# Reading each stack of queries or keys back from DRAM in one transfer of overlapping runs instead of two

## The chip, the cores and the metric

The kernel runs on one core of a Trainium2 chip. The metric is the device time of one execution in microseconds (us). Three runs of the kernel before give a median of 3047.06 us (3043.91 to 3050.0).

## What is computed

Two transformer-like blocks and two feed-forward stacks over one sequence of 2048 tokens with 128 channels. Cut to what matters here:

```python
def _attn(x, wq, wk, wv, wo, bq, bk, bv, bo):          # 16 heads of 8 dimensions, causal
    q, k, v = (x @ wq + bq), (x @ wk + bk), (x @ wv + bv)   # split into heads
    att = einsum('bhqd,bhkd->bhqk', q, k) * hd ** (-0.5)
    att = softmax(where(causal, att, -inf))
    return einsum('bhqk,bhkd->bhqd', att, v) @ wo + bo

x = x + _L0_attn_a_ref(_layernorm(x), ...)   # cumulative sums, stage a
x = x + _L0_ffn_ref(_layernorm(x), ...)      # 2 layers: causal attention, 8 experts (top 2), stage f
x = x + _L0_attn_b_ref(_layernorm(x), ...)   # attention without a mask, stage b
x = x + _L0_ffn_ref(_layernorm(x), ...)      # 2 layers again, stage g
```

There are five attention stages: f0, f1, b, g0, g1.

## The kernel before, in words

The 2048 tokens are worked on in 4 chunks of 512 (`CHUNKS`, `CH`). A projection computes q, k and v of a chunk. To have float32-like scores from bf16 products, each q and k is split into three bf16 parts, high, mid and low (0, 1, 2), and six products of parts are added: these are six groups of 8 rows (`HD`), stacked in 48 partitions of `m.q_stack` and `m.k_stack`, so that one matmul contracts over all of them. There are two such stacks, in partitions 0 to 47 (half b = 0, even heads) and 64 to 111 (half b = 1, odd heads). Row 48 of each is the shift row: in q_stack the negative row maximum, in k_stack ones.

The parts reach the stacks through DRAM, because the rows have to change partition. `write_part` (lines 670 to 678, and 936 to 945; `EarlyProjection.write` in the second layers) writes one part of q or k of a chunk into its slots of `q_parts` or `k_parts`; `Q_SLOTS` and `K_SLOTS` say which part is in which slot, and a part that stands in two slots is written to both by one transfer. The DRAM tensor has the slots outermost, then the 8 dimensions, the 16 heads, the 2048 tokens. `load_stacks` (lines 680 to 694 and 947 to 961; `EarlyProjection.load` from line 1241) reads a chunk and half of q and then of k back. Before, each takes two transfers: the four slots (32 partitions), then two slots again (16 partitions). Both count on one semaphore, and `arrived = 32 * (m.layers + 1)` is what TensorE waits for.

```python
queue.wait_ge(written[k][c % 2], 16 * 3 * (c // 2 + 1))
at = HALF * b
for n, first in ((SLOTS, 0), (AGAIN, again)):
    queue.dma_start(stack[at:at + n * HD, c, :, :],
                    dram.rearrange("r (hp b) s -> r b hp s", b=2)[first * HD:(first + n) * HD, b, :, cols])\
        .then_inc(arrived[b][c], 16)
    at += n * HD
```

Who issues what is written out by hand. In the full projections (`project_qkv` for f0 and b, `project_behind` for g0) SP issues the writes of all chunks and, for half 0, the loads of chunks 0 and 1; ACT issues chunk 0, half 1; GpSimd (POOL) chunk 1, half 1. The loads of chunks 2 and 3 are issued in the attention stage: in f0 and g0 by SP between its shifts (half 0) and by POOL between its masks (half 1), in b by both ahead of everything else. In the second layers (f1, g1, `EarlyProjection`) SP and POOL issue chunks 0 and 1 during the experts of the layer before, between SP's loads of the combine rows (line 2713), and chunks 2 and 3 in the attention stage. ScalarE reuses a slot of `parts` for chunk c only when the writes of chunk c - 2 have landed (`act.wait_ge(written[k][c % 2], ...)`, line 819), and SP, ACT and POOL wait for the same semaphores before a load.

In an attention stage TensorE works in the order of a planner (`Plan`): scans (line 1696) whose maxima VectorE takes (line 1856), a turn of the maxima (line 1716) and a shift on SP for every group of queries (lines 1928 and 1933), then scores (line 1734), exp on ScalarE (line 1804) and products with v (line 1755). TensorE waits for q_stack and k_stack of a chunk at their first use, and for the shift of a group at its first scores. In f0, f1, g0 and g1 the first four groups need chunk 0 alone; in b the first two groups are scanned against the keys of all four chunks, chunk after chunk.

Of the kernel before, what the change touches and what calls it, by code (L numbers as in the profile page):

```python
# [16 lines left out]
S = 2048  # L17
TILES = S // P
CH = 512
CHUNKS = S // CH  # L20
TPC = CH // P
HEADS, HD = 16, 8
# [11 lines left out]

Q_SLOTS = [0, 1, 2, 0]
K_SLOTS = [2, 1, 0, 0]
SLOTS = len(Q_SLOTS)
Q_AGAIN, K_AGAIN = 0, 1  # L40
AGAIN = 2
STACK = (SLOTS + AGAIN) * HD
PAIRS = HEADS // 2
HALF = P // 2
SHIFT_ROW = STACK
VD = HD + 1
# [9 lines left out]
class Steps:  # L56
# [5 lines left out]
    def __call__(self, instruction):  # L62
        self.n += 1
        instruction.then_inc(self.sem, 1)
        self.engine.wait_ge(self.sem, self.base + self.n)


def by_dim(ap):
# [559 lines left out]
def project_qkv(nc, m, n, buffers, layer=None, first_rows=None):  # L628
# [6 lines left out]
    with ExitStack() as ctx:  # L635
# [34 lines left out]
        def write_part(sp, c, k, part):  # L670

            dram, parts_of = ((m.q_dram, Q_SLOTS), (m.k_dram, K_SLOTS))[k]
            places = [g for g, of in enumerate(parts_of) if of == part]
# [6 lines left out]
        def load_stacks(queue, c, b):  # L680

            cols = slice(c * CH, (c + 1) * CH)
            for k, (stack, dram, arrived, again) in enumerate(((m.q_stack, m.q_dram, m.q_in, Q_AGAIN),
                                                               (m.k_stack, m.k_dram, m.k_in, K_AGAIN))):
                queue.wait_ge(written[k][c % 2], 16 * 3 * (c // 2 + 1))
                if c == CHUNKS - 1:
                    queue.wait_ge(v_ready, CHUNKS)
                at = HALF * b
                for n, first in ((SLOTS, 0), (AGAIN, again)):
                    queue.dma_start(stack[at:at + n * HD, c, :, :],  # L690
                                    dram.rearrange("r (hp b) s -> r b hp s", b=2)[first * HD:(first + n) * HD, b, :, cols])\
                        .then_inc(arrived[b][c], 16)
                    at += n * HD

        @block.gpsimd
        def _(pool):
            if first_rows:
                first_rows.powers(pool, BACK, 2)
            else:
                inverse_root(nc, pool, m, m.rstd[:, :], tmp[:, 0, :], var_ready, rstd_ready, 1)  # L700
            m.clear(pool, "finish", "experts", "rows", "w2")
            buffers.pad(nc, m)
            load_stacks(pool, 1, 1)

        @block.sync
        def _(sp):
            for c in range(CHUNKS):
                for part, ready in enumerate((high_ready, mid_ready, low_ready)):
                    for k in range(2):
                        sp.wait_ge(ready, 2 * c + k + 1)  # L710
                        write_part(sp, c, k, part)
                    if part == 0 and 0 < c <= EARLY:
                        load_stacks(sp, c - 1, 0)
# [87 lines left out]
        def _(act):  # L801
# [13 lines left out]
            for c in range(CHUNKS):  # L815
                for k in range(2):
                    act.wait_ge(mixed if mixing else qk_ready, 2 * c + k + 1)
                    if c >= 2:
                        act.wait_ge(written[k][c % 2], 16 * 3 * (c // 2))
                    if mixing:  # L820
                        nc.scalar.activation(parts[:, c % 2, k, 0, :], projected(c, k), ACT.Copy)\
                            .then_inc(high_ready, 1)
                    else:
                        nc.scalar.activation(parts[:, c % 2, k, 0, :], projected(c, k), ACT.Identity, bias=bias[k])\
                            .then_inc(high_ready, 1)
                if c == 1:
                    load_stacks(act, 0, 1)
                if c + 2 < CHUNKS:
                    copy_chunk(c + 2)
                for k in range(2):  # L830
                    act.wait_ge(rest_ready, 2 * c + k + 1)
                    nc.scalar.activation(parts[:, c % 2, k, 1, :], rest[:, k, :], ACT.Copy).then_inc(mid_ready, 1)
# [73 lines left out]
def project_behind(nc, m, n, buffers, layer, first_rows, attended, finish):  # L906

    src, end = m.x, CHUNKS - 1
    with ExitStack() as ctx:
# [26 lines left out]
        def write_part(sp, c, k, part):  # L936

            dram, parts_of = ((m.q_dram, Q_SLOTS), (m.k_dram, K_SLOTS))[k]
            places = [g for g, of in enumerate(parts_of) if of == part]
# [7 lines left out]
        def load_stacks(queue, c, b):  # L947

            cols = slice(c * CH, (c + 1) * CH)
            for k, (stack, dram, arrived, again) in enumerate(((m.q_stack, m.q_dram, m.q_in, Q_AGAIN),  # L950
                                                               (m.k_stack, m.k_dram, m.k_in, K_AGAIN))):
                queue.wait_ge(written[k][c % 2], 16 * 3 * (c // 2 + 1))
                if c == end:
                    queue.wait_ge(v_ready, CHUNKS)
                at = HALF * b
                for n, first in ((SLOTS, 0), (AGAIN, again)):
                    queue.dma_start(stack[at:at + n * HD, c, :, :],
                                    dram.rearrange("r (hp b) s -> r b hp s", b=2)[first * HD:(first + n) * HD, b, :, cols])\
                        .then_inc(arrived[b][c], 16)
                    at += n * HD  # L960

        @block.gpsimd
        def _(pool):
            load_stacks(pool, 1, 1)
            first_rows.powers(pool, BACK, 2)
            pool.wait_ge(finish.measured, CHUNKS)
            for name in ("searched", "exped", "drained", "projected"):
                pool.wait_ge(*attended[name])
            for done in attended["out"]:
                pool.wait_ge(*done)  # L970
            m.zero(pool, old)
            buffers.pad(nc, m)
            pool.wait_ge(m.named["h_padded"], len(buffers.layouts))
            pool.sem_inc(m.reset, 1)

        @block.sync
        def _(sp):
            for c in range(CHUNKS):
                for part in range(3):
                    for k in range(2):  # L980
                        if (c, part, k) == (end, 2, 1):
                            sp.wait_ge(low_ready, 2 * end + 1)
                            sp.wait_ge(m.reset, 2)
                        write_part(sp, c, k, part)
                    if part == 0 and 0 < c <= EARLY:
                        load_stacks(sp, c - 1, 0)
                    if c == 0 and part == 0:
                        finish.spread(sp, end)
                if c == 0:
                    finish.gather(sp, end)  # L990
# [136 lines left out]
class EarlyProjection:  # L1127
# [105 lines left out]
    def write(self, sp, c, k, part):  # L1233
        sp.wait_ge((self.high_ready, self.mid_ready, self.low_ready)[part], 2 * c + k + 1)
        dram, parts_of = ((self.m.q_dram, Q_SLOTS), (self.m.k_dram, K_SLOTS))[k]
        places = [g for g, of in enumerate(parts_of) if of == part]
# [5 lines left out]
    def load(self, queue, c, b):  # L1242
        m, cols = self.m, slice(c * CH, (c + 1) * CH)
        if c == 2:
            queue.wait_ge(*self.ones_back)
        for k, (stack, dram, arrived, again) in enumerate(((m.q_stack, m.q_dram, m.q_in, Q_AGAIN),
                                                           (m.k_stack, m.k_dram, m.k_in, K_AGAIN))):
            queue.wait_ge(self.written[k][c % 2], 16 * 3 * (c // 2 + 1))
            at = HALF * b
            for n, first in ((SLOTS, 0), (AGAIN, again)):  # L1250
                queue.dma_start(stack[at:at + n * HD, c, :, :],
                                dram.rearrange("r (hp b) s -> r b hp s", b=2)[first * HD:(first + n) * HD, b, :, cols])\
                    .then_inc(arrived[b][c], 16)
                at += n * HD

    def set_ones(self, pool):

# [382 lines left out]
def attention_heads(nc, m, n, buffers, projected, finish, rows_of, raw_weights, w2, stale, early, first_rows=None):  # L1640
# [7 lines left out]
    shift_moves = []  # L1648
    for g, (_, _, _, tiles) in enumerate(groups):
        shift_moves.append((2 if tiles == TPC else 4) + (shift_moves[g - 2] if g >= 2 else 0))  # L1650
    arrived = 32 * (m.layers + 1)
    m.layers += 1

    with ExitStack() as ctx:
# [21 lines left out]
        def _(pe):  # L1676
# [8 lines left out]
            def scan(i, g, p, parts):  # L1685
# [7 lines left out]
                for hp, t, width in parts:  # L1693
                    for b in range(2):
                        rows = slice(HALF * b, HALF * b + STACK)
                        last = nc.tensor.matmul(ps_scan[:, i % RING_A, b, at:at + width],  # L1696
# [22 lines left out]
            def scores(n_pair):  # L1719
# [10 lines left out]
                for i in range(QUAD // plan.banks(g)):  # L1730
                    pair = 2 * quad + k // 2 + i
                    for b in range(2):
                        rows = slice(HALF * b, HALF * b + STACK + 1)
                        last[b] = nc.tensor.matmul(ps_scores[(2 * n_pair + b) % RING_S][:, width * i + off:width * (i + 1)],  # L1734
# [1102 lines left out]
```

## Time and profile before

| what | value |
|---|---|
| median of three runs | 3047.06 us |
| the profiled execution | 3046.33 us |
| its span | 3044.6 us |
| TensorE busy | 2646.6 us (87%) |
| VectorE busy | 2598.8 us (85%) |
| ScalarE busy | 2249.2 us (74%) |
| GpSimd busy | 637.5 us (21%) |
| DMA over the span | 119.09 MB, mean 39 GB/s |

The span is the profiled execution seen from its first to its last instruction. In the rows, SPq, ACTq and POOLq are the engines' own issue of DMAs; a figure in brackets is the time in which the engine stood idle before the row, with what ended it. "us to landing" is from the issue to the last byte's arrival. The list of transfers groups them by size; the KB are those of one transfer.

### The profile page before, as it was taken

The numbers are of one execution on the slowest core, as the hardware profiler recorded it, in microseconds if no ns is written. First come the engines' busy times: TensorE is split into PE (matmuls) and PEld (weight loads), VectorE is DVE, ScalarE is ACT, GpSimd is POOL, SyncE is SP. The second block draws the span as 40 slices with busy tenths as digits, with TensorE's granted clock in tenths as the row PEclk, the third lists the DMA queues.
The fourth block names the chain that finished last, engine by engine and source line by source line (L and its number), as shares of the span: only waits on it lengthen the run. The fifth ranks groups of instructions, "written<-read, shape, count | busy, mean of one in ns | idle before, by whom it ended". The sixth has DMA issues, their size and how long they took to land. (4 is left out here: it accounts for less than half of the span.)

```text
span 3044.6 us, 71512 instructions
## 1 busy us (share of the span) xinstructions
PE 2646.6 (87%) x28144; PEld 1160.3 (38%) x28144; DVE 2598.8 (85%) x3528; ACT 2249.2 (74%) x4330; POOL 637.5 (21%) x1177
## 2 busy tenths in 40 slices
PE   3679999899799995689999999589999898899976
PEld 3432333677323334322222222232334775333325
DVE  4789998787899985799999999598997887899976
ACT  1258988676589884369999999378887675688874
POOL 5233211544321011100000000132102433321011
PEclk8779999999799997889999999799999998899998
DMA  1141000224300000410000000510001223300001
GB/s 34 53 101 39 27 23 16 73 56 97 71 27 16 18 9 24 116 27 11 17 9 17 9 16 9 138 33 29 15 13 34 66 66 89 65 28 16 13 16 28
DMA packets 109883, 119.09 MB, mean 39 GB/s; under 512 B 20726, under 2 KB 87660, under 8 KB 109548
## 3 DMA queue, kind: packets, MB, share of 16 engines
q1 hardware_dynamic: 102444, 98.21, 12.2%
q0 software_dynamic: 4608, 13.96, 2.2%
q8 instruction: 222, 3.64, 0.5%
q10 hardware_dynamic: 2496, 2.36, 0.3%
q14 instruction: 113, 0.93, 0.1%
HBM read 70.31 MB, written 43.78 MB: 37 GB/s over the span
## 5 line engine op out<-in xcount | busy, mean ns | idle before, releaser
L1804 ACT ACTIVATE h_probsg<-h_ps_lowg 128x512 f32<-128x512 f32 (+3 forms) x812 | 424.5, 551 | 108.5 <-PE h_ps_lowg L1734 70.7
L1804 ACT ACTIVATE h_probsf<-h_ps_lowf 128x512 f32<-128x512 f32 (+3 forms) x812 | 424.4, 550 | 107.3 <-PE h_ps_lowf L1734 68.5
L1804 ACT ACTIVATE h_probsb<-h_ps_lowb 128x512 f32<-128x512 f32 x683 | 389.2, 596 | 61.0 <-PE h_ps_lowb L1734 46.2
L1755 PE MATMUL h_ps_valuesg<-h_probsg,v_all 128*9 128x256 f32 (+2 forms) x4608 | 350.2, 376 | 25.9 <-POOL h_probsg L1917 19.0
L1755 PE MATMUL h_ps_valuesf<-h_probsf,v_all 128*9 128x256 f32 (+2 forms) x4608 | 349.0, 375 | 26.0 <-POOL h_probsf L1917 19.3
L1755 PE MATMUL h_ps_valuesb<-h_probsb,v_all 128*9 128x256 f32 x4096 | 317.9, 382 | 7.9 <-ACT h_drainedb L1813 3.1
L1856 DVE TENSOR_REDUCE h_maxima_0b<-h_ps_scanb 128x2 f32<-128x1024 f32 x256 | 292.5, 1213 | 6.7 <-PE h_ps_scanb L1696 6.7
L1856 DVE TENSOR_REDUCE h_maxima_2b<-h_ps_scanb 128x2 f32<-128x1024 f32 x256 | 292.6, 1214 | 5.1 <-PE h_ps_scanb L1696 5.1
L1856 DVE TENSOR_REDUCE h_maxima_0g<-h_ps_scang 128x2 f32<-128x1024 f32 x224 | 258.9, 1216 | 19.8 <-PE h_ps_scang L1696 19.1
L1856 DVE TENSOR_REDUCE h_maxima_0f<-h_ps_scanf 128x2 f32<-128x1024 f32 x224 | 258.6, 1216 | 18.6 <-PE h_ps_scanf L1696 18.0
L1804 ACT ACTIVATE h_probsf<-h_ps_highf 128x512 f32<-128x512 f32 (+3 forms) x404 | 224.0, 554 | 35.0 <-PE h_ps_lowf L1734 32.3
L1804 ACT ACTIVATE h_probsg<-h_ps_highg 128x512 f32<-128x512 f32 (+3 forms) x404 | 224.0, 555 | 34.7 <-PE h_ps_lowg L1734 32.2
L1917 POOL TENSOR_SCALAR_AFFINE_SELECT h_probsg<-h_probsg 128x128 f32<-128x128 f32 (+1 forms) x384 | 121.5, 330 | 610.9 <-ACT h_probsg L1804 603.8
L1917 POOL TENSOR_SCALAR_AFFINE_SELECT h_probsf<-h_probsf 128x128 f32<-128x128 f32 (+1 forms) x384 | 121.5, 330 | 574.9 <-ACT h_probsf L1804 568.2
L1696 PE MATMUL h_ps_scanf<-k_stack,q_stack 48*128 48x512 bf16 (+3 forms) x1280 | 217.5, 360 | 25.4 <-DVE h_maxima_0f L1856 7.9
L1696 PE MATMUL h_ps_scang<-k_stack,q_stack 48*128 48x512 bf16 (+3 forms) x1280 | 219.8, 364 | 22.6 <-DVE h_maxima_0g L1856 7.3
L1734 PE MATMUL h_ps_lowf<-q_stack,k_stack 49*128 49x256 bf16 (+2 forms) x1368 | 226.9, 286 | 10.3 <-DMA q_stack<-h_shiftsf 4.4
L1734 PE MATMUL h_ps_lowg<-q_stack,k_stack 49*128 49x256 bf16 (+2 forms) x1368 | 228.0, 287 | 7.8 <-ACT h_probsg L1804 2.6
L1696 PE MATMUL h_ps_scanb<-k_stack,q_stack 48*128 48x512 bf16 x1024 | 202.8, 393 | 21.6 <-DVE h_maxima_0b L1856 9.4
L1804 ACT ACTIVATE h_probsb<-h_ps_highb 128x512 f32<-128x512 f32 x341 | 203.4, 596 | 11.1 <-PE h_ps_lowb L1734 8.2
L1734 PE MATMUL h_ps_lowb<-q_stack,k_stack 49*128 49x256 bf16 x1366 | 200.2, 275 | 5.9 <-ACT h_probsb L1804 5.6
L1856 DVE TENSOR_REDUCE h_maxima_2g<-h_ps_scang 128x2 f32<-128x1024 f32 x160 | 185.5, 1218 | 14.5 <-PE h_ps_scang L1696 13.5
(465 smaller groups left out, 5240.6 us busy)
## 6 DMA issues: line engine op xcount, KB each, us to landing
q_stack<-combine_weights SPq DMA_DIRECT2D x64, 256.0 KB, 3.7
q_stack<-in_L_ffn_e_w SPq DMA_DIRECT2D x24, 256.0 KB, 3.3
q_stack<-q_parts SPq DMA_DIRECT2D x22, 256.0 KB, 5.5
k_stack<-k_parts SPq DMA_DIRECT2D x22, 256.0 KB, 7.4
attended<-h_drainedf SPq DMA_DIRECT2D x16, 256.0 KB, 2.3
attended<-h_drainedf SPq DMA_DIRECT2D x32, 128.0 KB, 2.0
attended<-h_drainedb SPq DMA_DIRECT2D x32, 128.0 KB, 1.9
attended<-h_drainedg SPq DMA_DIRECT2D x16, 256.0 KB, 2.3
```

Of the source, the lines that this page charges most:

```text
L1696: last = nc.tensor.matmul(ps_scan[:, i % RING_A, b, at:at + width], m.q_stack[rows, c, 2 * quad + hp, t * P:(t + 1) * P], m.k_stack[rows, ...
L1734: last[b] = nc.tensor.matmul(ps_scores[(2 * n_pair + b) % RING_S][:, width * i + off:width * (i + 1)], m.k_stack[rows, kb // TPC, pair, at ...
L1755: last = nc.tensor.matmul(ps_values[32 * j:32 * j + VD, low:high], m.v_all[:, kb, QUAD * quad + j, :], probs[:, (u + j % banks) % RING_P, ...
L1804: nc.scalar.activation(by_head(probs[:, of % RING_P, :], of), by_head(ps_scores[of % RING_S], of), ACT.Exp, scale=SOFTMAX_SCALE).then_inc( ...
L1856: nc.vector.tensor_reduce(found[:, :, low], now, AXIS_X, ALU.max).then_inc(freed, 1)
L1917: nc.gpsimd.affine_select(out=at, in_=at, compare_op=ALU.is_ge, fill=0.0, base=0, pattern=[[0, at.shape[1]], [1, P]], channel_multiplier=- ...
```

## The change

The high part's two places are moved to neighbouring or alternating slots, so that the six groups of 8 rows are overlapping runs of the four slots: for q three runs of two slots, each one slot on (0 0 | 0 1 | 1 2), for k two runs of three slots (2 0 1 | 0 1 0). A new function `stack_rows` builds an access pattern with the runs as its outermost step, and one transfer of 48 partitions takes the place of two. The semaphore counts 16 instead of 32 per load.

```diff
-Q_SLOTS = [0, 1, 2, 0]
-K_SLOTS = [2, 1, 0, 0]
+Q_SLOTS = [0, 0, 1, 2]
+K_SLOTS = [2, 0, 1, 0]
 SLOTS = len(Q_SLOTS)
-Q_AGAIN, K_AGAIN = 0, 1
-AGAIN = 2
-STACK = (SLOTS + AGAIN) * HD
+Q_RUNS, K_RUNS = (3, 2), (2, 3)
+STACK = 6 * HD
...
+def stack_rows(dram, runs, b, cols):
+
+    first = dram.rearrange("r (hp b) s -> r b hp s", b=2)[0:1, b, 0:1, cols]
+    count, places = runs
+    return bass.AP(first.tensor, first.offset, [[HD * HEADS * S, count], [HEADS * S, places * HD], [2 * S, PAIRS], [1, CH]])
...
                 queue.wait_ge(written[k][c % 2], 16 * 3 * (c // 2 + 1))
                 if c == CHUNKS - 1:
                     queue.wait_ge(v_ready, CHUNKS)
-                at = HALF * b
-                for n, first in ((SLOTS, 0), (AGAIN, again)):
-                    queue.dma_start(stack[at:at + n * HD, c, :, :],
-                                    dram.rearrange("r (hp b) s -> r b hp s", b=2)[first * HD:(first + n) * HD, b, :, cols])\
-                        .then_inc(arrived[b][c], 16)
-                    at += n * HD
+                queue.dma_start(stack[HALF * b:HALF * b + STACK, c, :, :], stack_rows(dram, runs, b, cols))\
+                    .then_inc(arrived[b][c], 16)
...
-    arrived = 32 * (m.layers + 1)
+    arrived = 16 * (m.layers + 1)
```

The same edit stands in both `load_stacks` and in `EarlyProjection.load`. In the built program the DRAM side of a load before is one run of 256 or 128 rows of 512 elements, against 32 or 16 partitions of 8 rows each; after, it is 3 runs of 128 rows for q and 2 runs of 192 rows for k, against 48 partitions of 8 rows each.

The instructions of SP in the first projection, where it loads chunk 0, half 0 between writes of chunk 1 (`q_parts` and `k_parts` are the DRAM tensors), before:

```order
36 L677 DMA q_parts<-p_partsf 128x2x512
37 L677 DMA k_parts<-p_partsf 128x2x512
38 L690 DMA q_stack<-q_parts 32x8x512
39 L690 DMA q_stack<-q_parts 16x8x512
40 L690 DMA k_stack<-k_parts 32x8x512
41 L690 DMA k_stack<-k_parts 16x8x512
42 L677 DMA q_parts<-p_partsf 128x512
43 L677 DMA k_parts<-p_partsf 128x512
```

and after the change:

```order
36 L683 DMA q_parts<-p_partsf 128x2x512
37 L683 DMA k_parts<-p_partsf 128x2x512
38 L694 DMA q_stack<-q_parts 48x8x512
39 L694 DMA k_stack<-k_parts 48x8x512
40 L683 DMA q_parts<-p_partsf 128x512
41 L683 DMA k_parts<-p_partsf 128x512
```

Two issues stand where four stood; nothing else has moved.

SP at the start of the attention stage f0, where loads of chunks 2 and 3 stand between the shifts of the first groups (`h_shiftsf` are the negated maxima), before:

```order
63 L1928 DMA q_stack<-h_shiftsf 1x8x128 x2
64 L690 DMA q_stack<-q_parts 32x8x512
65 L690 DMA q_stack<-q_parts 16x8x512
66 L690 DMA k_stack<-k_parts 32x8x512
67 L690 DMA k_stack<-k_parts 16x8x512
68 L1928 DMA q_stack<-h_shiftsf 1x8x128 x2
69 L690 DMA q_stack<-q_parts 32x8x512
70 L690 DMA q_stack<-q_parts 16x8x512
71 L690 DMA k_stack<-k_parts 32x8x512
72 L690 DMA k_stack<-k_parts 16x8x512
73 L1928 DMA q_stack<-h_shiftsf 1x8x128 x4
```

and after:

```order
59 L1922 DMA q_stack<-h_shiftsf 1x8x128 x2
60 L694 DMA q_stack<-q_parts 48x8x512
61 L694 DMA k_stack<-k_parts 48x8x512
62 L1922 DMA q_stack<-h_shiftsf 1x8x128 x2
63 L694 DMA q_stack<-q_parts 48x8x512
64 L694 DMA k_stack<-k_parts 48x8x512
65 L1922 DMA q_stack<-h_shiftsf 1x8x128 x4
```

The shifts keep their places relative to the loads. The waits and the instructions of the other engines are the same, but for the loads that ACT and POOL issue, which go from four to two in the same way.

## Rows read from the trace of the kernel before

**Rows 1.** The page's first part: busy us (share of the span) and instructions.
```profile
PE 2646.6 (87%) x28144; PEld 1160.3 (38%) x28144; DVE 2598.8 (85%) x3528; ACT 2249.2 (74%) x4330; POOL 637.5 (21%) x1177
```
**Rows 2.** Transfers of the whole run: engine, op, count, KB each, us to landing.
```profile
q_stack<-q_parts SPq DMA_DIRECT2D x22, 256.0 KB, 5.5
...
k_stack<-k_parts SPq DMA_DIRECT2D x22, 128.0 KB, 8.1
```
**Rows 3.** DMA of 1395 to 1405 us: packets; queue with packets, MB, share; transfers.
```profile
DMA packets 161, 0.15 MB, mean 15 GB/s; under 512 B 32, under 2 KB 160, under 8 KB 160
...
q1 hardware_dynamic: 160, 0.13, 4.0%
...
attended<-h_drainedb SPq DMA_DIRECT2D x1, 128.0 KB, 2.0
q_stack<-h_shiftsb SPq DMA_DIRECT2D x4, 0.5 KB
```
**Rows 4.** DMA of 791 to 803 us (POOL's loads go by q0).
```profile
q0 software_dynamic: 512, 1.57, 73.3%
...
q1 hardware_dynamic: 32, 0.00, 0.4%
...
q_stack<-h_shiftsf SPq DMA_DIRECT2D x2, 2.0 KB
```
**Rows 5.** SP in order of time, first projection and start of f0: start us, us.
```profile
141.24 1.44 SPq L690 DMA_DIRECT2D q_stack<-q_parts  x2
...
152.18 1.20 SPq L690 DMA_DIRECT2D q_stack<-q_parts  x2
...
165.16 1.48 SPq L1928 DMA_DIRECT2D q_stack<-h_shiftsf  x2
166.69 1.26 SPq L690 DMA_DIRECT2D q_stack<-q_parts  x2
```
**Rows 6.** ACT and PE in order of time, the same stretch.
```profile
152.25 1.26 ACT L824 ACTIVATE p_partsf<-p_ps_qkf,vecs_dh 128x512 bf16<-128x512 f32 x2 [1.14 <-DMA q_parts<-p_partsf]
...
156.78 0.61 PE L1696 MATMUL h_ps_scanf<-k_stack,q_stack 48*128 48x128 bf16 x4 [5.96 <-issue]
...
190.40 0.39 PE L1734 MATMUL h_ps_lowf<-q_stack,k_stack 49*128 49x512 bf16 x1
```
**Rows 7.** DMA of 141.5 to 145.5 us, SP's queue and ACT's.
```profile
q1 hardware_dynamic: 772, 0.74, 62.9%
q10 hardware_dynamic: 381, 0.37, 37.4%
```
**Rows 8.** SP and PE in order of time, start of b.
```profile
1263.08 1.32 SPq L690 DMA_DIRECT2D q_stack<-q_parts  x2
...
1305.94 0.61 PE L1696 MATMUL h_ps_scanb<-k_stack,q_stack 48*128 48x512 bf16 x2 [0.61 <-DVE h_maxima_2b L1856]
```
**Rows 9.** ACT, POOL, SP and PE in order of time, start of g0.
```profile
1924.70 1.27 ACTq L957 DMA_DIRECT2D q_stack<-q_parts  x2
...
1937.86 1.16 POOL L957 DMA_DIRECT2D q_stack<-q_parts  x2 [35.70 <-DMA q_parts<-p_partsg]
...
1967.86 1.25 SPq L957 DMA_DIRECT2D q_stack<-q_parts  x2
...
1988.74 0.39 PE L1734 MATMUL h_ps_lowg<-q_stack,k_stack 49*128 49x512 bf16 x1
```
**Rows 10.** SP and POOL in order of time, experts of the first layer of f.
```profile
697.99 1.26 SPq L1251 DMA_DIRECT2D q_stack<-q_parts  x2
...
703.18 0.59 SPq L2713 DMA_DIRECT2D q_stack<-combine_weights  x1
...
725.54 1.29 POOL L2327 TENSOR_TENSOR q_stack<-q_stack 128x512 f32<-128x512 f32 x1 [0.68 <-ACT q_stack L2658]
```
**Rows 11.** SP and PE in order of time, start of f1.
```profile
807.50 1.25 SPq L1251 DMA_DIRECT2D q_stack<-q_parts  x2
...
824.75 0.38 PE L1734 MATMUL h_ps_lowf<-q_stack,k_stack 49*128 49x512 bf16 x1
```

More of the change, by code:

```diff
@@ L682, in load_stacks @@
             cols = slice(c * CH, (c + 1) * CH)
-            for k, (stack, dram, arrived, again) in enumerate(((m.q_stack, m.q_dram, m.q_in, Q_AGAIN),
-                                                               (m.k_stack, m.k_dram, m.k_in, K_AGAIN))):
+            for k, (stack, dram, arrived, runs) in enumerate(((m.q_stack, m.q_dram, m.q_in, Q_RUNS),
+                                                               (m.k_stack, m.k_dram, m.k_in, K_RUNS))):
                 queue.wait_ge(written[k][c % 2], 16 * 3 * (c // 2 + 1))
@@ L949, in load_stacks @@
             cols = slice(c * CH, (c + 1) * CH)
-            for k, (stack, dram, arrived, again) in enumerate(((m.q_stack, m.q_dram, m.q_in, Q_AGAIN),
-                                                               (m.k_stack, m.k_dram, m.k_in, K_AGAIN))):
+            for k, (stack, dram, arrived, runs) in enumerate(((m.q_stack, m.q_dram, m.q_in, Q_RUNS),
+                                                               (m.k_stack, m.k_dram, m.k_in, K_RUNS))):
                 queue.wait_ge(written[k][c % 2], 16 * 3 * (c // 2 + 1))
@@ L954, in load_stacks @@
                     queue.wait_ge(v_ready, CHUNKS)
[L955 to L960, printed above, removed]
+                queue.dma_start(stack[HALF * b:HALF * b + STACK, c, :, :], stack_rows(dram, runs, b, cols))\
+                    .then_inc(arrived[b][c], 16)
         @block.gpsimd
@@ L1245, in load @@
             queue.wait_ge(*self.ones_back)
-        for k, (stack, dram, arrived, again) in enumerate(((m.q_stack, m.q_dram, m.q_in, Q_AGAIN),
-                                                           (m.k_stack, m.k_dram, m.k_in, K_AGAIN))):
+        for k, (stack, dram, arrived, runs) in enumerate(((m.q_stack, m.q_dram, m.q_in, Q_RUNS),
+                                                           (m.k_stack, m.k_dram, m.k_in, K_RUNS))):
             queue.wait_ge(self.written[k][c % 2], 16 * 3 * (c // 2 + 1))
[L1249 to L1254, printed above, removed]
+            queue.dma_start(stack[HALF * b:HALF * b + STACK, c, :, :], stack_rows(dram, runs, b, cols))\
+                .then_inc(arrived[b][c], 16)
     def set_ones(self, pool):
```

## Prediction

> **What bounds the kernel now.** I read the page first: TensorE is busy for 2646.6 us, 87% of the span [rows 1], so a transfer matters only where TensorE is left without work. Such places lie where an attention stage begins, since its first scores need the stacks. Then I read the list of transfers: the first piece of a q stack and half lands 5.5 us after its issue on SP, the second piece of k after 8.1 us [rows 2]. Last I read the queue and the engines in order of time at each start. In the first projection SP issues the loads of chunk 0 at 141.24 us and of chunk 1 at 152.18 us; a shift, the row that the scores wait for, goes out at 165.16 us, and the loads of chunk 2 at 166.69 us, right behind it [rows 5]. ScalarE waits 1.14 us for a slot of the writes at 152.25 us, the search begins at 156.78 us, and the scores of the third group at 190.40 us [rows 6]. So the loads now fit in with a few us to spare.
>
> **What the change removes.** 160 transfers become 80, with the same 1 KB rows and bytes. The two issues of q take 1.44 us of a queue [rows 5], and I give those of k as much; half goes, 1.44 us per chunk and half. On SP it lies beside the search. On ACT it comes once in each of the three full projections, 4.3 us in all at most; I credit 0, since at 152.25 us ScalarE ends on a wait for the writes, not on its own work, and keep the 4.3 us as the gain of the rival below. The moved slots change only which two places a high part is written to: same rows, same shape, cost 0. The order of the terms in a product changes and no TensorE instruction does.
>
> **What it adds: fewer DMA engines.** Look at completions. In a window with one write of 128 rows and four shifts of 2 pieces there are 160 packets, 32 of them small [rows 3]. The write makes 128, the shifts 4 x 2 = 8, so 24 are completions: 16 for the write and 2 for each shift. In another window two shifts of 8 pieces show 32 packets [rows 4]: 16 pieces and 16 completions, 8 for each. A transfer thus reports from as many engines as its leading count gives, up to 16. The loads of before lead with 256 or 128 rows in DRAM and 32 or 16 in SBUF: 16 engines. Those of the change lead in DRAM with the runs, 3 for q and 2 for k, against 48 partitions. I take it that both sides are cut at their leading counts, so that q runs on 3 engines and k on 2, and that every transfer of SP and ACT starts at the same first engine (rival 2 is that they do not). The rows do not prove it, as each shift has no more pieces than engines. The Trainium skill ("DMA: Bandwidth & Descriptors", section "Why a DMA increments its semaphore by 16 and not by 1") says so outright: the number of engines is the largest up to 16 that divides the slowest dimension of both sides, and the hardware queues take the lowest-numbered ones. By that rule the sum below stands.
>
> The price per packet: with loads of both halves in flight, 772 + 381 packets take 62.9% + 37.4% of 16 engines for 4 us [rows 7], 64.2 us / 1153 = 55.7 ns. With loads of one half alone it is 73.3% of 16 x 12 us for 1.57 MB [rows 4], 92 ns per KB. I take 55.7: the slower figure comes where 16 engines press into the same 48 partitions, and 2 or 3 will not. Lower end: 160 packets, 32 of them small, in 4.0% of 160 us [rows 3] is 40 ns, so a 1 KB row takes at most 50. A q load puts 384/3 = 128 packets on the first engine, a k load 384/2 = 192: 320 x 55.7 ns = **17.8 us** for a chunk and half, against 2.7 us now (the 768 packets are 48 on each of 16). Call it p; p = 16.0 at 50 ns and 29.3 at 92. On an engine a queue is served in order, so writes and shifts issued behind a load wait for it. GpSimd's own loads I take as lying on others and beside.
>
> *First projection.* Both halves of chunk 0 (SP and ACT) share the engines: done at 141.2 + 2p + 2 = 179, and with them the writes of chunk 1 queued behind. ScalarE's wait at 152.25 ends 27 us later, and the search starts 27 later. SP then issues chunk 1 (p), shift 0, chunk 2 (p), shift 1, chunk 3 (p), shift 2, each shift behind a load. The third group's scores start at 141.2 + 5p + 7 (landing, writes and issues between) = 237 instead of 190.4 [rows 6]: **+47 us** (5p - 42).
>
> *The middle stage (b)* needs the keys of all chunks to find its first maximum. Loads begin at 1263.08 us, the scans of chunk 3 at 1305.94 [rows 8]. Now 1263.1 + 5p + 6 = 1358: **+52 us** (5p - 37).
>
> *The projection behind (g, first layer).* GpSimd waits at 1937.86 us for the writes of chunk 1 before its own loads [rows 9], and first_scale, the normalised chunk 3 and the search are behind that wait. ACT's loads begin at 1924.70 [rows 9] and SP's behind: + 2p + 2 = 1962.3, so 24.4 us more. SP's loads of chunk 2 move from 1967.86 to 1992.3, chunk 3 follows, + 2p + 2 = 2029.9 against scores of the third group at 1988.74 [rows 9]: **+41 us** (4p - 30).
>
> *Second layers (f and g).* Chunks 0 and 1 come during the experts. Behind them the combine rows for the multiply at 725.54 us wait: issued at 703.18 [rows 10] behind two halves begun at 697.99, they land near 736. GpSimd loses 11 us, with two buffers of slack before ScalarE and TensorE wait; I charge 4 (0 to 15). Chunks 2 and 3 go out at 807.50 us in one burst, the next shift must pass 2p: 807.5 + 2p + 2 = 845 instead of scores at 824.75 [rows 11]: 20 us (2p - 15). Together **+24 us**, twice.
>
> Sum: 47 + 52 + 41 + 48 = 188 us. The profiled execution took 3046.3 us, 0.7 below the median of the runs: 3235 us. At 50 ns: 38 + 43 + 34 + 2 x (17 + 3) = 155, 3202 us; at 92 ns: 104 + 110 + 87 + 2 x (43 + 15) = 417, 3464 us.
>
> **Rivals.** (1) *All 16 engines still serve a load*, and only issues go. For it: nothing in the rows shows a large transfer narrowed. Against it: 3 and 2 runs cannot be dealt evenly to 16, and completions follow the leading count [rows 3, 4]. The time is 3047 less 0 to 4.3 us, 3045; with an earlier release of the writes at the three starts, 2 to 3 us each, 3038. It decides wherever a load alone lands within 8.1 us as now. The same skill page, section "Rules for kernel authors", advises to coalesce many small transfers into one; by that advice this would be the outcome. (2) *The queues use different engines*, or q and k do: p counts once where two halves start together. First projection 4p - 44 = 27, b 4p - 38 = 33, g 3p - 30 = 23, second layers 20 each: +123, 3170 us. For it: ACT's queue has its own line in the rows [rows 7]. Against: both fill all 16 engines together there. (3) *Few engines at the slow price*: 3464 us. For it: 92 ns is what loads of one half show [rows 4]; against it, the crowding above.
>
> **Numbers.** The forecast with its own range of 3202 to 3300 us has 0.58; the same with longer knock-on stalls, up to 3440, 0.05; rival 2 0.13; rival 3 0.08; rival 1 0.16, of it 0.10 with no change and 0.06 faster. I leave out rival 1, and of rival 3 the end above 3440, with a part of 0.04: range 3130 to 3440 us. 0.2% is 6 us, about what a measurement of this kernel can tell. Slower 0.84, the same 0.10, faster 0.06.
>
> **What would show it.** Landing times of a q load near 9 us and a k load near 13 us alone, above 20 where two share; a DMA share of about 3/16 in slices with high delay; the first search near 184 us; scores waiting for a shift in every attention stage; b's scans waiting for k_stack. I am wrong if a load lands within 8 us, if landing times are long but TensorE starts as before, or if the stalls are made good later in a stage, which the 87% [rows 1] hardly allows.

## The result and the profile after

The changed kernel takes 3244.69 us (median of 4 runs, 3241.29 to 3249.77) against 3046.98 us for the kernel before in the same session: ratio 1.065, 95% interval 1.063 to 1.0671, so 197.7 us slower. The forecast was 3235 us in 3130 to 3440. The profiled execution took 3249.77 us, its span 3248.0.

The page of the profile after: TensorE's and the DMA's slices, and the queues (packets, MB, share of 16 engines). It answers to [rows 1].

```profile
PE 2663.1 (82%) x28144; PEld 1160.9 (36%) x28144; DVE 2604.4 (80%) x3528; ACT 2249.4 (69%) x4330; POOL 648.9 (20%) x1147
...
PE   4549999897689995539999999469999897699986
...
PEclk8759999998799997759999999779999998799997
DMA  1131000213210000130000000220000213200001
...
DMA packets 124248, 119.35 MB, mean 37 GB/s; under 512 B 35091, under 2 KB 102025, under 8 KB 123913
...
q1 hardware_dynamic: 101146, 98.20, 10.0%
q0 software_dynamic: 20448, 14.22, 2.3%
```

TensorE has 16.5 us more of busy time and 187 us more without work, so the loss is nearly all waiting. The number of its instructions is the same; behind the waits they run at the lower clock level for longer: from 226 to 235 us of after the granted clock is 0.50 of full speed (1.2 GHz), and the scores at 240.32 us below take 0.60 us where those of [rows 6] take 0.39; over the span the clock is 0.908 against 0.938. The forecast has no term for this. The bytes are nearly the same (119.35 MB against 119.09) and fewer transfers carry them, yet GpSimd's queue (q0) has 20448 packets where the page of before has 4608.

The list of transfers after, which answers to [rows 2]:

```profile
q_stack<-q_parts SPq DMA_DIRECT2D x22, 384.0 KB
...
q_stack<-q_parts POOLq DMA_DIRECT2D x15, 384.0 KB, 14.5
k_stack<-k_parts POOLq DMA_DIRECT2D x15, 384.0 KB, 17.7
```

GpSimd's loads land after 14.5 and 17.7 us; in the list of before the two transfers of each load land after 4.7 to 7.6. The list has no landing for SP's, so the landing times that the prediction named as its first sign cannot be read for SP.

How few engines there are shows in the DMA of 150 to 160 us of after, while one half of chunk 0 comes by SP's queue (q1) and the other by ScalarE's (q10). The first two rows cut the stretch in 40 slices.

```profile
DMA  1221222211221222221111111111111111111111
GB/s 70 74 74 70 74 74 74 74 70 70 74 74 61 66 70 74 74 74 57 45 49 49 49 49 49 49 49 45 45 49 49 49 49 49 49 49 49 49 41 49
DMA packets 581, 0.59 MB, mean 59 GB/s; under 512 B 6, under 2 KB 581, under 8 KB 581
## 3 DMA queue, kind: packets, MB, share of 16 engines
q1 hardware_dynamic: 326, 0.33, 9.5%
q10 hardware_dynamic: 255, 0.26, 7.3%
```

It is 74 GB/s first and then 49, for both queues together. I read it as three engines and then two, at 24.6 GB/s each; the two shares, 16.8% of 16 engines together, lie between 3/16 and 2/16. With [rows 7] at 1.11 MB in 4 us, 278 GB/s, this is the loss in one row. A 1 KB packet then costs an engine 1024 B / 24.6 GB/s = 41.6 ns.

SP in order of time, first projection of after, against [rows 5]:

```profile
141.07 7.06 SPq L694 DMA_DIRECT2D k_stack<-k_parts  x1
148.17 16.03 SPq L683 DMA_DIRECT2D q_parts<-p_partsf  x1
164.25 0.63 SPq L683 DMA_DIRECT2D k_parts<-p_partsf  x1
...
171.58 0.72 SPq L694 DMA_DIRECT2D q_stack<-q_parts  x1
172.34 1.30 SPq L694 DMA_DIRECT2D k_stack<-k_parts  x1
173.68 19.13 SPq L683 DMA_DIRECT2D q_parts<-p_partsf  x1
...
199.51 0.77 SPq L694 DMA_DIRECT2D q_stack<-q_parts  x1
```

The issue of the write behind a load takes 16.03 and 19.13 us where that of the next write takes 0.63. Over the whole program 34 single issues of SP take more than 3 us each, 325 us together; before there is none. So the writes behind a load do not only land late, SP itself stands still at them.

The engines in order of time at the starts: ScalarE and TensorE in f0, against [rows 6]; TensorE's scans in b, [rows 8]; GpSimd and TensorE in g0, [rows 9]; TensorE in f1, [rows 11].

```profile
171.64 1.26 ACT L826 ACTIVATE p_partsf<-p_ps_qkf,vecs_dh 128x512 bf16<-128x512 f32 x2 [21.64 <-DMA q_parts<-p_partsf]
...
176.18 0.61 PE L1690 MATMUL h_ps_scanf<-k_stack,q_stack 48*128 48x128 bf16 x4 [26.47 <-DVE h_ps_valuesf L1814]
...
226.75 0.60 PE L1728 MATMUL h_ps_lowf<-q_stack,k_stack 49*128 49x512 bf16 x1 [12.89 <-DMA q_stack<-h_shiftsf]
...
240.32 0.60 PE L1728 MATMUL h_ps_highf<-q_stack,k_stack 49*128 49x512 bf16 x1 [2.64 <-DMA q_stack<-h_shiftsf]
...
1428.86 1.04 PE L1690 MATMUL h_ps_scanb<-k_stack,q_stack 48*128 48x512 bf16 x4 [20.78 <-DMA k_stack<-k_parts]
...
1442.44 1.03 PE L1690 MATMUL h_ps_scanb<-k_stack,q_stack 48*128 48x512 bf16 x4 [5.38 <-DMA k_stack<-k_parts]
...
2095.24 1.36 POOL L957 DMA_DIRECT2D q_stack<-q_parts  x1 [55.59 <-DMA q_parts<-p_partsg]
...
2162.14 0.60 PE L1728 MATMUL h_ps_highg<-q_stack,k_stack 49*128 49x512 bf16 x1 [4.24 <-DMA q_stack<-h_shiftsg]
...
907.93 0.61 PE L1728 MATMUL h_ps_lowf<-q_stack,k_stack 49*128 49x512 bf16 x1 [5.66 <-DMA q_stack<-h_shiftsf]
```

In b the scans wait for the keys of chunk 2 up to 1428.86 us and for those of chunk 3 up to 1442.44, the row to set against 1305.94 in [rows 8].

Where the 203.4 us between the spans arise is read from TensorE's rows in order of time: the start of a stage's first scan and the end of its last scores, after less before. The "experts" column runs from the last scores to the next layer's first scan; b and g0 include the projection ahead of them. The same subtraction is made for every experiment:

| us later | f0 | experts f | f1 | b | g0 | experts g | g1 | sum |
|---|---|---|---|---|---|---|---|---|
| forecast | 47 | 4 | 20 | 52 | 41 | 4 | 20 | 188 |
| after | 52.1 | 14.7 | 15.6 | 55.1 | 36.4 | 9.7 | 20.0 | 203.6 |
| k alone | 31.4 | 5.0 | 10.3 | 33.0 | 17.5 | 1.2 | 11.1 | 109.5 |
| q alone | 23.1 | 2.6 | 7.6 | 25.4 | 14.0 | 0.5 | 9.2 | 82.4 |
| chunks 0, 1 alone | 32.6 | 12.0 | 1.3 | 31.1 | 21.6 | 10.9 | 0.7 | 110.2 |
| experts' loads alone | -0.1 | 12.0 | 1.2 | 0.0 | -4.2 | 13.1 | 0.0 | 22.0 |
| deviation first | 53.9 | 8.4 | 15.4 | 55.7 | 34.4 | 6.7 | 19.3 | 193.8 |
| GpSimd's alone | 2.6 | 0.1 | 8.3 | 14.7 | 0.7 | -2.6 | 9.0 | 32.8 |
| 8 KB pieces | 46.4 | 11.4 | 15.5 | 48.1 | 26.1 | 7.3 | 24.4 | 179.2 |

The rows are named by the form that was changed; "8 KB pieces" is the run with the overlapping transfer in the 8 KB layout. A single profile holds such a term to about 4 us, as the terms of the two kernels closest to the one before show (two transfers in either layout, -4 to 4).

### The profile page after: what moved, and what is told of

Its sections match the earlier page's. It is cut to its first block and busy times, and to the rows that moved or that the text cites. A ratio compares the mean times of both kernels' runs of the same rounds, so it can differ in the third digit from the quotient of the medians.

```text
span 3248.0 us, 71432 instructions
## 1 busy us (share of the span) xinstructions
PE 2663.1 (82%) x28144; PEld 1160.9 (36%) x28144; DVE 2604.4 (80%) x3528; ACT 2249.4 (69%) x4330; POOL 648.9 (20%) x1147
## 2 busy tenths in 40 slices
DMA packets 124248, 119.35 MB, mean 37 GB/s; under 512 B 35091, under 2 KB 102025, under 8 KB 123913
## 3 DMA queue, kind: packets, MB, share of 16 engines
q1 hardware_dynamic: 101146, 98.20, 10.0%
q0 software_dynamic: 20448, 14.22, 2.3%
q8 instruction: 222, 3.64, 0.5%
## 5 line engine op out<-in xcount | busy, mean ns | idle before, releaser
L1850 DVE TENSOR_REDUCE h_maxima_0f<-h_ps_scanf 128x2 f32<-128x1024 f32 x224 | 259.5, 1217 | 26.2 <-PE h_ps_scanf L1690 25.4
L1690 PE MATMUL h_ps_scanb<-k_stack,q_stack 48*128 48x512 bf16 x1024 | 202.9, 395 | 75.1 <-DMA k_stack<-k_parts 38.1
L1728 PE MATMUL h_ps_lowg<-q_stack,k_stack 49*128 49x256 bf16 (+2 forms) x1368 | 229.9, 289 | 23.7 <-DMA q_stack<-h_shiftsg 17.8
L1798 ACT ACTIVATE h_probsb<-h_ps_highb 128x512 f32<-128x512 f32 x341 | 203.4, 596 | 12.0 <-PE h_ps_lowb L1728 9.2
## 6 DMA issues: line engine op xcount, KB each, us to landing
q_stack<-q_parts POOLq DMA_DIRECT2D x15, 384.0 KB, 14.5
k_stack<-k_parts POOLq DMA_DIRECT2D x15, 384.0 KB, 17.7
```

The costliest lines, as they stand in the source:

```text
L1798: nc.scalar.activation(by_head(probs[:, of % RING_P, :], of), by_head(ps_scores[of % RING_S], of), ACT.Exp, scale=SOFTMAX_SCALE).then_inc( ...
L1850: nc.vector.tensor_reduce(found[:, :, low], now, AXIS_X, ALU.max).then_inc(freed, 1)
```

## The experiments

All but the two with six slots keep the changed kernel's new slots. A function chooses the form of each load by stage, stack (`k` is 0 for q and 1 for k), chunk `c` and half `b`: "one" is the change's overlapping transfer, "two" the two transfers of before. TensorE's waits count accordingly. Most diffs show what it returns. Each measured time is compared with the kernel before of its own session (3044.45 to 3046.98 us).

### Is it the engines at all?

Two transfers again, in the new slots:

```diff
-    return "one"
+    return "two"
```

> The changed kernel with its new slot order, but each stack and half read back in two transfers again (32 and 16 rows). Engines theory (the loss is the transfers' spread over 3 or 2 of the 16 DMA engines, nothing else of the change): all of it goes, 3047 us within 6. Rival (the new order of the slots in DRAM, or in the stack, costs something of itself, such as a write of the high part that takes two places next to each other for q and two places apart for k): 3060 or more, in the extreme the whole 3245.

Measured: 3045.42 us, ratio 0.9996 (0.9986 to 1.0006). The slots cost nothing; all of the loss is in the form of the load.

A transfer for each run, 3 of 16 rows for q and 2 of 24 for k:

```diff
-    return "one"
+    return "runs"
```

which reads the stack (cut)

```python
spans = [(g, g + runs[1]) for g in range(runs[0])]
...
pieces = [((hi - lo) * HD, rows[lo * HD:hi * HD, b, :, cols]) for lo, hi in spans]
```

> The same rows in the same order as in the changed kernel, the overlapping ones read again too, but a transfer of its own for each run: three of 16 rows for q, two of 24 rows for k (so 16 and 12 engines by the greatest divisor). Five issues where the changed kernel has two, the same 768 packets. Engines theory: 3047 to 3065 us (an issue more than before on SP, POOL and ACT for each chunk and half costs its 0.1 to 1 us, hidden nearly everywhere). Rival (reading overlapping rows, or 768 separate 1 KB pieces in this order, is what is slow): near 3245.

Measured: 3056.50 us, ratio 1.003 (1.0018 to 1.0041). Neither the rows read twice nor their order is slow: the same rows cost 10 us with five issues and 198 us with two.

Six slots written out, one transfer of 48 rows in a row:

```diff
-Q_SLOTS = [0, 0, 1, 2]
-K_SLOTS = [2, 0, 1, 0]
+Q_SLOTS = [0, 0, 0, 1, 1, 2]
+K_SLOTS = [2, 0, 1, 0, 1, 0]
...
-        pieces = [(STACK, stack_rows(dram, runs, b, cols))]
+        pieces = [(STACK, dram.rearrange("r (hp b) s -> r b hp s", b=2)[:, b, :, cols])]
```

> Six slots are written out (high in three places, mid in two, low in one), and each stack and half is read back in one transfer of 48 rows in a row: one transfer as in the changed kernel, but no outer dimension of 3 or 2. Engines theory: all 16 engines take part, 3035 to 3060 us; the writes carry half as much again (3 MB more in 5 stages), beside other work. Rival (one transfer a stack is slow by itself, since 48 rows come on one queue entry instead of two): 3200 or more.

Measured: 3058.40 us, ratio 1.0048 (1.0031 to 1.0065). One transfer a stack is not slow by itself. This is the change's own number of transfers with a leading 48 in place of 3 or 2, at 12 us over before instead of 198. Its queue row shows the larger writes, 10.5 MB more than the 98.20 of after, not the 3 that I expected:

```profile
q1 hardware_dynamic: 111980, 108.69, 13.1%
```

### How the loss is made up of q and k

```diff
-    return "one"
+    return "one" if k else "two"
```

> Only the k stacks are read in one transfer (outer dimension 2), q in two. Engines theory: the shared first engine has 192 packets of k and 48 of q for a chunk and half instead of 320, p = 14.1 us where 18.8 us fits the 52 us of the first projection; by the terms of the prediction f0 5p-42 = 28, b 5p-37 = 33, g0 4p-30 = 26, second layers 2p-15 = 13 each, experts 7 each: 127 us, so 3174 (3150 to 3200). Rival (the cost is by transfers, not by packets on the first engine, so that each of the two stacks brings half): 3146 us. Rival (q's wait alone matters, since it is issued first and gates the scans): under 3080 us.

Measured: 3152.86 us, ratio 1.0352 (1.0335 to 1.0369), 106.6 us. The low end of what the engines theory allowed, and the rival by transfers (3146) is near too. The DMA of 150 to 155 us, with the same two queues in flight as above:

```profile
GB/s 49 49 49 49 49 49 49 49 49 49 49 49 49 49 49 41 49 49 49 41 49 49 49 49 49 49 49 49 49 49 49 49 49 49 49 49 41 49 49 41
DMA packets 236, 0.24 MB, mean 48 GB/s; under 512 B 0, under 2 KB 236, under 8 KB 236
...
q1 hardware_dynamic: 118, 0.12, 6.8%
q10 hardware_dynamic: 118, 0.12, 6.8%
```

It is a flat 49 GB/s, half by each queue. Two queues with engines of their own would have 98, so SP's and ScalarE's k loads share one pair. The 74 falling to 49 of after is then q's three engines and k's two. The share says the same: 13.6% of 16 engines is 2.2 of them. That is the forecast's assumption, shown for these two queues.

```diff
-    return "one"
+    return "two" if k else "one"
```

> Only the q stacks are read in one transfer (outer dimension 3), k in two. Engines theory with a shared first engine and a threshold (what the cover hides comes off once): 128 packets of q and 48 of k on it for a chunk and half, 10.3 us where k alone had 14.1: f0 5p-42 = 10, b 5p-37 = 15, g0 4p-30 = 11, second layers 5 each, experts 2 each, 50 us in all, so 3096 (3075 to 3110). Rival (q and k cost apart from each other, and add up): what k alone left of the whole, 198 - 107 = 91 us, so 3138. Rival (each has its engines to itself, and only the slower of the two is waited for): under 3060 us, since q would then be done before k in the old form's time plus 6 us.

Measured: 3131.84 us, ratio 1.0286 (1.0267 to 1.0306), 86.9 us. My 50 us fell; the rival that adds up (91) stood. In the table q alone and k alone give 54.5 us in f0 against 52.1 of both, 58.4 against 55.1 in b, 31.5 against 36.4 in g0. A slack as large as the forecast's, taken off in each of the two runs and once in the whole, would leave the sums well under the whole; they are not, so there is no such slack for a shorter load to hide in.

### Which loads, and through what chain

```diff
-    return "one"
+    return "one" if c < EARLY else "two"
```

> The one-transfer form only for chunks 0 and 1 of every stage, chunks 2 and 3 in two transfers. By the prediction: the second layers' attention terms (15.6 and 20.0 us in the trace of the changed kernel) come from chunks 2 and 3 alone and go; the experts' 24 us stay; of f0, b and g0 (52, 55, 36) the part ahead of the first scan stays (19 to 27, 18, 19.5) and that behind it shrinks: about 24 + 65 + a third of the other 78 = 115, so 3161 us (3130 to 3190). Rival (all is lost at the first loads, the rest only follows): 3230 or more. Rival (chunks 2 and 3 hold nearly all of it): under 3100.

Measured: 3154.08 us, ratio 1.035 (1.0329 to 1.0371). The terms came as said: f1 and g1 lose 1.3 and 0.7 us, the experts 12.0 and 10.9, and f0, b and g0 keep 85.3 of their 143.6.

```diff
-    return "one"
+    return "one" if stage in (1, 4) and c < EARLY else "two"
```

> The one-transfer form only in the second layers (f1 and g1), and there only for chunks 0 and 1, which are read back during the experts. Theory (the experts lose time of their own, through a chain that these loads start: SP is held in its issues, the writes and rows behind them are late, GpSimd's load waits and the deviation behind it is late): the 14.7 and 9.7 us that the trace of the changed kernel shows there come back whole, 3071 us (3065 to 3078). Rival (the experts' loss is the experts being out of step after a late attention stage, or is paid by something else of the change): 3046 to 3055 us.

Measured: 3067.77 us, ratio 1.0072 (1.0049 to 1.0096), 22.8 us. The experts' loss arises in their own loads. The waits of 730 to 830 us of after (engine and line, waited for: us in total, times, longest) show its chain:

```profile
DVE k_stack L1169 <- POOL rstd L1159: 15.5, 1, 15.5
PE e_ps_turnf L1176 <- DVE k_stack L1169: 15.1, 2, 15.0
POOL q_stack L1247 <- DMA q_parts<-k_stack: 11.9, 1, 11.9
```

and SP there:

```profile
755.81 9.09 SPq L1247 DMA_DIRECT2D q_stack<-q_parts  x1
764.94 5.96 SPq L1247 DMA_DIRECT2D k_stack<-k_parts  x1
770.94 8.02 SPq L2707 DMA_DIRECT2D q_stack<-combine_weights  x1
```

A write of chunk 1 is behind SP's loads, as I read it; GpSimd waits 11.9 us for it ahead of its own load (L1247); the deviation (L1159) is queued behind that wait; VectorE normalises and TensorE turns in order, so both stand for 15 us. To test the link at GpSimd, its load was put behind the deviation:

```diff
-NEXT_LOAD_BY_POOL = 25
+NEXT_LOAD_BY_POOL = 26
```

> The changed kernel, with GpSimd's load of chunk 1 in the experts issued one step later, behind the deviation of the last but one chunk instead of ahead of it. Theory (the experts' 15 and 10 us come from that deviation, queued behind GpSimd's wait for the late write): 15 to 24 us of the 198 go, 3221 to 3230 us. Rival (they come from SP: late rows of weights or late writes, that TensorE and VectorE wait for in any order): 3240 to 3247 us.

Measured: 3237.53 us, ratio 1.0627 (1.0606 to 1.0647), 192.6 us: between the two theories, and only 5 us less of a loss than the changed kernel's 197.7, with overlapping intervals. The waits of this kernel, 725 to 825 us, show why it is so little:

```profile
POOL q_stack L2347 <- DMA q_stack<-combine_weights: 15.2, 2, 8.2
...
DVE k_stack L1197 <- POOL rstd L1187: 8.6, 1, 8.6
PE e_ps_turnf L1204 <- DVE k_stack L1197: 8.6, 1, 8.6
```

GpSimd's wait for the write is gone, and it waits 15.2 us for combine rows instead, which SP issues late behind the same loads. The deviation is still behind it. The wait for it is 8.6 us instead of 15.5. In the table the experts lose 15.1 us instead of 24.4, so GpSimd's order carries 9 us at most, which is little beside the 4 us of a term; the rest I put down to what else SP is late with, above all these rows, which no run took apart.

Only GpSimd's 15 of the 40 pairs in one transfer:

```diff
-    return "one"
+    return "one" if b and c else "two"
```

> The one-transfer form only in GpSimd's loads (the second half of chunks 1 to 3, in one place SyncE's), 15 of the 40 pairs; SyncE and ScalarE load in two transfers. Theory (what costs is SyncE held in its issues on engines that it shares with ScalarE, with writes and shifts behind; GpSimd's transfers go to engines of their own and land 10 us later, which only b's scans and each stage's second chunk see): 0 to 5 us a stage, 3050 to 3070. Rival (the loss goes by the pairs in this form, 15 of 40): 3045 + 74 = 3120.

Measured: 3079.36 us, ratio 1.0112 (1.0097 to 1.0128), 34.9 us: over what I said, under the 74 of a share by pairs. b (14.7 us) sees the late landing. Its scans' group on this kernel's page, which after has at 38.1 us of waits for k_stack:

```profile
L1716 PE MATMUL h_ps_scanb<-k_stack,q_stack 48*128 48x512 bf16 x1024 | 202.6, 393 | 37.0 <-DMA k_stack<-k_parts 16.8
```

In f1 (8.3 us) another transfer suffers, the move of the attended values. The DMA of 800 to 830 us, and ScalarE:

```profile
q1 hardware_dynamic: 1998, 2.10, 38.2%
q0 software_dynamic: 1568, 1.28, 30.9%
...
attended<-h_drainedf SPq DMA_DIRECT2D x2, 256.0 KB, 10.1
k_stack<-k_parts POOLq DMA_DIRECT2D x1, 384.0 KB, 22.5
```

```profile
824.77 0.60 ACT L1833 ACTIVATE h_drainedf<-h_ps_valuesf 128x512 f32<-128x512 f32 x1 [3.64 <-DMA attended<-h_drainedf]
```

The attended values land after 10.1 us (the same two moves after 6.3 and 6.0 in before), and ScalarE, which needs their buffer for the next drain, waits 3.64 us; what the rest of the 8.3 us is this does not show. GpSimd's loads are all that differs from the run with two transfers, so they do not lie beside the others.

### By the packet or by the byte, and a better kernel

The heads' order in the columns of the q and k weights is changed once, and DRAM is laid out by chunk and half, so that a row of a stack is 8 KB in one piece. First with two transfers (cut):

```diff
-        self.q_dram = nc.dram_tensor("q_parts", [SLOTS * HD, HEADS, S], BF16, kind="Internal").ap()
+        self.q_dram = nc.dram_tensor("q_parts", [CHUNKS, SLOTS * HD, HEADS, CH], BF16, kind="Internal").ap()
...
-    return ap.rearrange("p (h d) -> p d h", d=HD)
+    return ap.rearrange("p (hp b d) -> p d b hp", d=HD, b=2)
...
-        rows = dram.rearrange("r (hp b) s -> r b hp s", b=2)
+        rows = dram[c][:, b * PAIRS:(b + 1) * PAIRS, :]
```

> DRAM laid out by chunk and by half (the heads' order in the columns of the weights changed once at the start), so that a row of a stack is one piece of 8 KB instead of eight of 1 KB; read back in two transfers of 32 and 16 rows, the new slot order. Writes still go out in pieces of 1 KB. Theory (on 16 engines the read back is near no bound: 1 KB pieces go at 24 GB/s an engine, 389 GB/s in all, and what is left on the path is the landing of a transfer, 5 to 8 us): small gain, 3035 to 3045 us. Rival (fewer, larger pieces halve the landing, and each of the five stages starts 3 us earlier, GpSimd's too): 3025 us or less. Rival (writes into rows that are 16 KB apart clash, or nothing was to be had): 3045 or more.

Measured: 3050.68 us, ratio 1.002 (1.001 to 1.003). No gain: larger pieces on all 16 engines take nothing off the path, and why it is a few us slower was not pursued.

The same layout with the overlapping transfer, 3 and 2 engines:

> The same layout with one transfer of overlapping runs, so 3 and 2 engines as in the changed kernel, but pieces of 8 KB. If an engine's rate is by bytes (24.6 GB/s, as with 1 KB pieces): 3230 to 3250 us. If the price is by piece (42 ns each, an eighth of the pieces): 3047 to 3070 us. Between them, an engine at 27 GB/s (as large pieces may do) gives 67 us * 0.9 in f0 and so on: 3220 us.

Measured: 3224.35 us, ratio 1.0574 (1.0552 to 1.0597). Nearly all by the byte. The DMA of 160 to 162 us, where SP's k load is under way in the first half (40 slices of 50 ns):

```profile
GB/s 0 164 164 0 0 0 0 164 164 0 0 0 0 164 164 0 0 0 0 164 164 0 0 0 0 164 164 102 205 328 369 532 451 348 307 369 369 328 635 328
```

Two pieces of 8 KB come every six slices, 0.3 us: 55 GB/s, or 27 from each of two engines, where 1 KB pieces have 49 and 24.5. That is the third case of the expectation, worth 18 of the 198 us and no more. SP is held much less in this kernel, at 22 issues over 3 us, 128 us together, against 34 and 325 us, and yet 180 us are lost. So the hold of SP's issues is not what the loss goes by; how long the loads themselves take is nearly unchanged.

Six slots in that layout, against the run before this one (cut):

```diff
-        pieces = [(STACK, stack_rows(dram[c], runs, b))]
+        pieces = [(STACK, dram[c][:, b * PAIRS:(b + 1) * PAIRS, :])]
```

> The same layout, six slots written out, one transfer of 48 rows of 8 KB for a stack and half on 16 engines: two issues fewer in each load, half as much again written. Theory: as the six slots with 1 KB pieces (0.48% slower than before) less what larger pieces bring, 3040 to 3055 us. Rival (the loss of that form came from 48 rows on one entry, not from the writes): 3045 with either, no difference to the 1 KB form.

Measured: 3057.40 us, ratio 1.0039 (1.0025 to 1.0053), as the six slots with 1 KB pieces. Whether its 13 us come from the larger writes or from a transfer of 48 rows on one entry these two do not tell apart. None of the variants beats the kernel before; two transfers in either order of slots are the best form measured.

## Why the prediction was right, point by point

- **Few engines, shared by both queues**: right, by the 74 and 49 GB/s and the flat 49 of k alone. The Trainium skill's rule ("DMA: Bandwidth & Descriptors", section "Why a DMA increments its semaphore by 16 and not by 1") held for SP's and ScalarE's queues. The Trainium skill's advice on the same page to coalesce many small transfers ("Rules for kernel authors"), which rival 1 leaned on, speaks of transfers under 64 KB. Those here have 128 KB and more, so it does not bear on this case; one transfer a stack brought nothing even without the narrow spread (six slots, 3058.40 us against 3045.42 with two). The number of transfers is not what counts: the form with 200 of them (3056.50 us) is 188 us faster than the change with 80. Rival 2 falls with the flat 49 and rival 3 with the 41.6 ns.
- **The size: two errors that cancel, which is luck.** The forecast took 55.7 ns a packet, p = 17.8 us, and slack of 42, 37 and 30 us in f0, b and g0. A packet costs 41.6 ns where these two queues have the engines to themselves, so p is 320 x 41.6 = 13.3 us. By the same formulas f0 would have lost 24.6, b 29.6 and g0 23.2 us; they lost 52.1, 55.1 and 36.4. With the second layers at 11.6 + 4 each, the whole would have been 109 us, 3155 us, 90 us short of what was measured. The other error is the small time beside the loads. In f0 the forecast gave it 7 us (141.2 + 5p + 7); the third group's scores began at 240.32 us, so that with 13.3 us a load it is 32.5. If every load took 13.3 us, the slack would be 66.6 - 52.1 = 14.5 us in f0, 11.5 in b and 16.8 in g0; the next point shows that some loads took longer, and how the 32.5 us divide was not measured. The run with q alone is what found this, since a slack is taken off once and not twice: 10 us were expected in f0 and 23.1 came.
- **"GpSimd's own loads I take as lying on others and beside"**: wrong, and part of why 13.3 us is too little. In f0 of after, the one load in flight on SP's and ScalarE's queues (issued at 171.58) ends SP's hold only at 192.8, 21 us on, 8 more than p. In that stretch:

```profile
DMA packets 1979, 1.50 MB, mean 72 GB/s; under 512 B 1127, under 2 KB 1785, under 8 KB 1977
...
q0 software_dynamic: 1312, 0.80, 16.2%
q1 hardware_dynamic: 665, 0.67, 11.0%
```

  GpSimd's load brings 1312 packets of 610 bytes on average, and SP's queue moves 0.67 MB in 21 us, 32 GB/s, less than the 49 of k alone. Two shorter stretches of after, 180 to 184 us with GpSimd's load in flight and 226 to 230 us without one, show that they go together:

```profile
q0 software_dynamic: 91, 0.37, 26.4%
q1 hardware_dynamic: 51, 0.05, 4.5%
```

```profile
q1 hardware_dynamic: 257, 0.26, 18.2%
```

  SP's queue moves 51 packets in 4 us beside GpSimd's and 257 without; even the k loads of both queues on their two engines moved 190 in the 4 us from 160 us on. That the two clash on the same engines is how I read it; GpSimd's form alone costs 35 us, but a run with only SP and ScalarE in the new form was not made, so how much of the 198 is their clash stays open.
- **"On an engine a queue is served in order, so writes and shifts issued behind a load wait for it"**: right in effect, and more than that: SP itself is held at the issue, 16.03 and 19.13 us. The landmarks show both errors of size. ScalarE's wait ended and the search began 19.4 us later where 27 were forecast (176.18 us for 184); 2p + 2 with 13.3 us gives 169.8 us for the end of that wait, and it was 171.64. The third group's scores then began at 240.32 (237). In b the stages before have cost 82.4 us, and the scans of chunk 3 began 54.1 us later besides (52). In g0 137.5 us are lost before it begins: GpSimd's wait ended at 2095.24, 19.9 us later besides (24.4), the third group's scores 35.9 later (41).
- **The experts**: the term that was mis-sized, 4 us a layer (0 to 15) against 14.7 and 9.7. I followed the combine rows into the buffers of the multiply. In f the longest wait of TensorE there, 15.0 us, came through GpSimd's order instead: a wait for a late write, the deviation behind it, VectorE and TensorE in order behind that. Undoing that order gave back 9 us at most; where the other 15 lie stays open.
- **Second layers' attention**: 20 us forecast, 15.6 and 20.0 measured, and only chunks 2 and 3 make it, as said (1.3 and 0.7 us without them). The mechanism was half of it: GpSimd's loads alone give 8.3 and 9.0, in part through ScalarE's wait for the drained values' buffer (3.64 us of it in f1), which the forecast did not name.
- **Removed issues**: no run shows a gain from them, as credited.

## What to carry to other kernels

Before two transfers are made one, count the engines that each will use: see whether the new outermost count divides as well as the old one. Here 3 and 2 in place of 32 and 16 turned 278 GB/s into 74 and 49. Writing all six slots out (12 us slower than before) or a transfer for each run (10 us slower) keeps clear of it, but neither beats the two transfers of before. When costing a slow transfer, list what its queue issues behind it, then what each waiting engine has behind that wait: part of the experts' 24 us lay two engines away from the load. And test a sum by halving its cause: a formula "5p less a slack" can be right in total and wrong in both parts.

## What I had not expected of the hardware

- An engine's issue of a DMA can itself take up to 19.1 us when a large transfer on 2 or 3 engines is ahead: 34 single issues of SP over 3 us with the overlapping transfer, none with two transfers, none with a transfer for each run, one each, of 3.1 and 3.4 us, in the two runs with six slots.
- One engine moved 24.6 GB/s with 1 KB pieces and 27 with 8 KB pieces: between these two sizes the piece hardly mattered where the engines were few.
- GpSimd's loads with the overlapping form come in far smaller packets: 20448 in all against 4608, and 14.22 MB against 13.96; they land after 14.5 and 17.7 us and slow transfers of other queues (attended values 10.1 us against 6.3 and 6.0). With a leading 48 in DRAM the same loads have 4128 packets on that queue in all and land after 7.1 and 9.3 us.
- The two stacks' losses add up to nearly the whole (82.4 + 109.5 = 191.9 of 203.6 us).
